# Three edits of one planning step in a fused attention and expert kernel: order of inverse roots, row copy and image differences on GpSimd, and a split wait on TensorE

## The chip, the cores and the metric

The kernel runs on one core of one Trainium2 chip. The metric is the device time of one launch in microseconds (us). Three runs of the kernel before gave 1237.05, 1237.48 and 1237.81 us; the median, 1237.48, is the time before. A smaller time is better.

## The reference

Sixteen images of 256 x 256 are turned into edge maps, 77 text rows are looked up in a table and set behind each, and the 333 x 256 sequence goes through windowed attention and a two-of-eight expert layer, each behind a layer norm and with a residual.

```python
def reference(x, x_txt, ...):
    h = _L0_tok_ref(x)          # clip(|x[i,j]-x[i+1,j+1]| + |x[i+1,j]-x[i,j+1]|, 0, 1)
    h = jnp.concatenate([h, _L0_txt_ref(L0_txt_weight, x_txt)], axis=1)
    h = h + _L0_attn_ref(_layernorm(h, axis=-1), Wq, bq, Wk, bk, Wv, bv, Wo, bo, pos_bias)
    h = h + _L0_ffn_ref(_layernorm(h, axis=-1), gate_w, w1, w2, w3)
    return h
# _layernorm: (x - mean) / sqrt(var + 1e-5)
# attention: 16 heads of 16; windows of 128 rows, every 64 rows, and one at the end; per window
#   softmax(q k^T / 4 + pos_bias) v, added up and divided by the number of windows over each row
# expert layer: softmax gate over 8 experts, the best two, silu(x w1) * (x w3) w2, weighted sum
```

## The kernel before

The program has two stages. The first, up to about 725 us, takes the images in a software pipeline; the second is a loop of expert tiles, which the change doesn't touch.

**Steps and slots.** Every engine runs the same outer loop over steps b = -3 to 17 and, in it, 20 slots k = 0 to 19 (5 windows x 4 groups of 4 heads). The order of the work is written out by hand: in slot k of step b an engine's code has the attention of image b and pieces of the images before and behind it. The flags say which pieces exist: `att` (image b is in attention), `tail` (image b-1 is being finished), `tail2` (image b-2 is sent to the expert slots), `proj` (image b+1 gets q, k and v), `inp` (image b+2 is normalised) and `pre` (image b+3 is made from pixels). So `pre` ends after step 12, `inp` after step 13 and `proj` after step 14. Engines meet only through semaphores; slots aren't barriers, and an engine that has nothing to wait for runs ahead.

**Attention in each slot.** TensorE computes the scores of group k (L1273), transposes the probabilities of group k-3 (L1284) and multiplies those of k-4 with the values (L1300). VectorE adds the bias and takes the maximum (L980), ScalarE takes the exponential (L741) and copies the transposed probabilities out of PSUM (L734); for one group in four VectorE makes that copy (L989), in slots 18, 2, 6, 10 and 14. Once per window TensorE turns the raw output (L753 on ScalarE, then L1409), VectorE scales it (L1001, L1008), TensorE turns it back (L1259, in slot 18 behind the gate matmuls), ScalarE copies it (L760) and GpSimd adds it into ctxT (L581).

**What the change touches, in slots 12 to 19.**
- GpSimd (`pool`), slot 12: the two image differences diag and anti (L631, L633), which wait for the pixels. Slot 13: `inverse_roots` (L506 to L518), 14 small instructions of which each waits for the one before; they wait for the statistics of the finished image b-1 (`ln2_step`) and of the coming image b+2 (`ln1_step`). Slot 15: ctxT (L581). Slot 16: the copy of the rows (L654), which waits for `rows0_ready`. Slot 18: h_res (L667), which waits for the normalised image b+2 (`xn_ready`), then the sum of the absolute differences (L672, waits for `conv_step`) and the clipped image (L677).
- VectorE (`dve`), slot 12: statistics of image b-1 (L810, L813). Slot 13: the absolute values of diag and anti (L1114). Slot 14: two of three value banks (`add_v`, L968). Slot 15: the rows of image b-1 (L818, three instructions, wait for `rstd_ready`). Slot 16: the third value bank (L968), then xn of image b+2 (L818, three). Slot 17: L980 and the scaling into ctx_q. Slot 18: L980 and the copy L989.
- TensorE (`pe`), slot 17: the transposes of the rows (L1390), six into the two halves of m_bank, behind one wait for the rows and one for all three values of image b+1, since these are read from m_bank. Slot 18: the gate matmuls (L1397), which wait for ScalarE's copy of these transposes (L728). Slot 0: the transposes of xn (L1329).
- SyncE loads the pixels of the next image when `diffs_ready` has counted the two differences.

## Time and profile before

| | |
|---|---|
| median of 3 runs | 1237.48 us |
| the profiled execution | 1235.95 us |
| its span, first to last instruction | 1233.8 us |
| TensorE busy (matmul) | 1146.1 us, 93% |
| VectorE busy | 837.9 us, 68% |
| ScalarE busy | 707.0 us, 57% |
| GpSimd busy | 595.6 us, 48% |
| one batch, L1409 to L1409, batches 2 to 12 | 40.9 us |

The profile is of one execution. Busy times are of instructions, without the waits; an engine's idle time is put down to what it waited for last. In the timelines below a line is one or several instructions of the same kind in a row: start, duration, engine, line of the code, what is written and read, how many, and in brackets the idle time before it and who ended it. GpSimd is called POOL, VectorE DVE, TensorE PE and ScalarE ACT. A batch is named by its step b.

### The profile page before, as it was taken

How to read it: one execution, taken by the hardware profiler on the slowest of the kernel's cores; microseconds unless marked ns; L12 is line 12 of the kernel's file. 1: busy time of each engine (PE TensorE's matmuls, PEld its weight loads, DVE VectorE, ACT ScalarE, POOL GpSimd, SP SyncE). 2: the span in 40 equal slices, each digit the busy share in tenths (PEclk: the TensorE clock that was granted, in tenths of full speed). 3: DMA queues.
4: the chain of work that ended last, by engine and by line, in shares of the span. 5: the costliest groups of instructions: out<-in, count | busy, mean ns of one | idle time of the engine just before them, and what ended most of it. 6: DMA issues, size and time to landing. Idle time of an engine off the chain costs nothing.

```text
span 1233.8 us, 34479 instructions
## 1 busy us (share of the span) xinstructions
PE 1146.1 (93%) x10510; PEld 944.6 (77%) x10511; DVE 837.9 (68%) x4279; ACT 707.0 (57%) x1979; POOL 595.6 (48%) x751
## 2 busy tenths in 40 slices
PE   2499999999999999999998798999999999999995
PEld 1366766676667667666766698999999999999995
DVE  3488899899989899989888774444444444444442
ACT  1399999999999999999999721111111111111110
POOL 7655656765676567656653362223232332323232
PEclk9799999999999999999999998999999999999998
DMA  4654446554554355434535332232333323233332
GB/s 134 180 162 122 139 136 188 142 147 131 153 144 114 96 151 147 111 99 129 148 99 173 112 101 45 47 47 47 48 47 50 47 47 47 47 47 49 49 47 30
DMA packets 98394, 123.31 MB, mean 100 GB/s; under 512 B 15544, under 2 KB 87416, under 8 KB 95192
## 3 DMA queue, kind: packets, MB, share of 16 engines
q1 hardware_dynamic: 75880, 89.96, 26.7%
q0 software_dynamic: 18576, 24.47, 12.0%
q10 hardware_dynamic: 3808, 7.34, 1.9%
q8 instruction: 59, 0.97, 0.3%
q14 instruction: 71, 0.58, 0.2%
HBM read 69.35 MB, written 46.07 MB: 94 GB/s over the span
## 4 chain that ended last, share of the span: by engine, by line
PE 70%; DVE 7%; ACT 7%; POOL 7%; issue 4%; SPq 2%; DMA 1%; ACTq 0%; POOLq 0%; DVEq 0%
PE t_bank L1197 13%; PE s_bank L1197 13%; PE o_bank L1212 13%; PE m_bank L1245 7%; PE t_bank L1284 6%; PE o_bank L1300 5%; ACT probs L741 4%; PE s_bank L1273 4%; DVE probs L980 3%; PE m_bank L1239 3%; PE m_bank L1397 2%; PE m_bank L1186 2%; PE o_bank L1259 1%; PE o_bank L1409 1%; ACT probsT L734 1%
## 5 line engine op out<-in xcount | busy, mean ns | idle before, releaser
L741 ACT ACTIVATE probs<-probs,neg_max 128x128 f32<-128x128 f32 x1280 | 402.4, 398 | 2.1 <-DVE neg_max L980 2.1
L980 DVE CUSTOM_DVE_ANT_0 probs<-s_bank,nbias 128x128 f32<-128x128 f32 x1280 | 293.4, 284 | 56.6 <-PE s_bank L1273 51.2
L699 ACT ACTIVATE v_all<-s_bank 128x512 f32<-128x512 f32 x91 | 54.4, 598 | 284.5 <-PE s_bank L1197 284.4
L1284 PE MATMUL t_bank<-ident,probs 128*128 128x128 f32 x1280 | 194.1, 274 | 0.2 <-ACT probs L741 0.2
L1212 PE MATMUL o_bank<-stacks,v_all 128*128 x728 | 172.7, 381 | 0.6 <-issue 0.5
L537 POOL DMA_INDIRECT out_dram<-wq_sb,nbias x46 | 75.0, 1629 | 176.5 <-DVE wq_sb L924 159.4
L734 ACT ACTIVATE probsT<-t_bank 128x512 f32<-128x512 f32 x240 | 142.0, 592 | 31.1 <-PE t_bank L1284 28.7
L537 POOL DMA_INDIRECT out_dram<-wk_sb,nbias x45 | 74.9, 1663 | 170.8 <-DVE wk_sb L924 161.9
L1212 PEld LDWEIGHTS o_bank<-stacks,v_all 128*128 128x128 f32 x728 | 131.6, 191 | 15.8 <-issue 1.7
L930 DVE TENSOR_TENSOR v_all<-v_all,t_bank 128x512 f32<-128x512 f32 x91 | 62.5, 687 | 119.0 <-PE t_bank L1197 119.0
L1300 PE MATMUL o_bank<-probsT,v_all 128*32 128x128 f32 x2560 | 136.3, 285 | 7.1 <-ACT probsT L734 4.0
L1273 PE MATMUL s_bank<-stacks 96*128 96x128 bf16 x1280 | 126.2, 221 | 16.7 <-DMA stacks<-qk_parts 16.7
L1273 PEld LDWEIGHTS s_bank<-stacks 96*128 96x128 bf16 x1280 | 93.6, 98 | 59.9 <-issue 24.8
L1284 PEld LDWEIGHTS t_bank<-ident,probs 128*128 128x128 f32 x1280 | 134.4, 141 | 0.8 <-ACT probs L741 0.5
L551 POOL DMA_INDIRECT expert_slots<-rows,slot_i x96 | 96.4, 1004 | 39.6 <-issue 39.6
L693 ACT ACTIVATE v_all<-m_bank 128x256 f32<-128x256 f32 x91 | 34.5, 383 | 131.5 <-PE m_bank L1186 131.5
L980 DVE DVE_READ_ACCUMULATOR2_ANT neg_max<- 128x1 f32 x1280 | 103.9, 81 | 0.0
L1300 PEld LDWEIGHTS o_bank<-probsT,v_all 128*32 128x32 f32 x2560 | 50.5, 108 | 62.3 <-issue 47.9
L1197 PEld LDWEIGHTS s_bank<-v_all,parts_flat 128*128 128x128 f32 x736 | 90.8, 195 | 4.0 <-ACT v_all L693 1.9
L1197 PE MATMUL s_bank<-v_all,parts_flat 128*128 128x128 f32 x736 | 91.7, 279 | 1.0 <-ACT v_all L693 1.0
L1197 PE MATMUL t_bank<-v_all,parts_flat 128*128 128x128 f32 x736 | 90.6, 277 | 0.0
L1197 PEld LDWEIGHTS s_bank<-v_all,probs 128*128 128x128 f32 x720 | 87.4, 192 | 2.3
(169 smaller groups left out, 1988.2 us busy)
## 6 DMA issues: line engine op xcount, KB each, us to landing
stacks<-qk_parts SPq DMA_DIRECT2D x192, 166.5 KB
qk_parts<-parts_flat SPq DMA_DIRECT2D x192, 83.2 KB
nbias<-expert_slots SPq DMA_DIRECT2D x91, 129.0 KB, 2.1
w_sb<-in_L_ffn_w_dram ACTq DMA_DIRECT2D x14, 512.0 KB, 3.8
v_all<-v_all SPq DMA_DIRECT2D x64, 96.0 KB
x_here<-in_x_dram SPq DMA_DIRECT2D x16, 256.0 KB
out_dram<-h_res SPq DMA_DIRECT2D x16, 256.0 KB
stacks<-in_L_ffn_w_dram SPq DMA_DIRECT2D x8, 512.0 KB, 6.0
```

What stands on the lines that cost most here:

```text
L537: pool.indirect_dma_start(out[:, :], bass.IndirectOffsetOnAxis(g_rows[r][:, D + 1:D + 2].bitcast(I32), 0), y_sb[r], None, compute_op=ALU.a ...
L551: pool.indirect_dma_start(slots_dram[:, :], bass.IndirectOffsetOnAxis(slot_i[0:n, kk, j:j + 1], 0), rows[0:n, kk, j, :], None).then_inc(sc ...
L734: act.activation(probsT[:, r, :], t_bank[:, r, :], ACT.Copy).then_inc(pT_by_act, 1)
L741: ins = act.activation(seg, seg, ACT.Exp, bias=neg_max[:, r, i:i + 1], scale=-1.0)
L930: dve.tensor_tensor(hidT[r % 2], hidT[r % 2], t_bank[:, r % 2, :], ALU.mult).then_inc(hid_ready, 1)
L980: ins = dve.tensor_tensor_reduce(probs[:, r, i * WIN:(i + 1) * WIN], s_bank[:, k % 2, i * WIN:(i + 1) * WIN], nbias[:, h, :], 1.0, BIG, AL ...
L1197: mm = pe.matmul(bank[:, par, n * P:(n + 1) * P], up_w[par][:, m, a, n * P:(n + 1) * P], gxT[par][:, a * P:(a + 1) * P], start=(a == 0), s ...
L1212: mm = pe.matmul(o_bank[:, r % 2, 0:D], hidT[r % 2][:, a * P:(a + 1) * P], w2_sb[:, bass.ds(e, 1), a, :].rearrange("p o n -> p (o n)"), st ...
L1245: mm = pe.matmul(m_bank[:, c, 0:S], (wq_sb if n == 0 else wk_sb)[:, a, c * P:(c + 1) * P], xT[:, a, :], start=(a == 0), stop=(a == C - 1))
L1273: mm = pe.matmul(s_bank[:, k % 2, i * WIN:(i + 1) * WIN], q_stack[par][0:KROWS, h, lo:lo + WIN], k_stack[par][0:KROWS, h, lo:lo + WIN], st ...
L1284: mm = pe.transpose(t_bank[:, (k - 3) % 2, i * WIN:(i + 1) * WIN], probs[:, r, i * WIN:(i + 1) * WIN], ident[:, :])
L1300: mm = pe.matmul(o_bank[32 * i:32 * i + 32, vp, g * WIN:(g + 1) * WIN], v_win[bp][:, w, c0:c0 + 2 * HD], probsT[:, (k - 4) % 2, i * WIN:(i ...
```

## The change

On GpSimd the inverse roots move from slot 13 to slot 12 (in steps from 0 on; before that they stay in 13), the row copy of slot 16 keeps its slot, and the image differences move from slot 12 to slot 16, behind the row copy (steps -3 and -1 keep slot 12, step -2 keeps 17). On VectorE the absolute values of the differences move from slot 13 to slot 17 in steps from 0 on. On TensorE the row transposes into the first half of m_bank wait for two of the three values and those into the second half for the third.

```diff
@@ gpsimd, step @@
-                    if pre and k == (17 if b == -2 else 12):
-                        pool.wait_ge(x_in, b3 * 64 + 64)
-                        ...
-                        pool.tensor_tensor(diag[:, :, :], x_here[:, :, 0:IMG], x_below[:, :, 1:IMG + 1],
-                                           ALU.subtract).then_inc(diffs_ready, 1)
-                        pool.tensor_tensor(anti[:, :, :], x_below[:, :, 0:IMG], x_here[:, :, 1:IMG + 1],
-                                           ALU.subtract).then_inc(diffs_ready, 1)
-                    if (tail or inp) and k == 13:
+                    if (tail or inp) and k == (13 if b < 0 else 12):
                         ...
                         inverse_roots(0 if inp else NT, 2 * NT if tail else NT, b + 2)
-                    if b == B and k == 14:
-                        pool.wait_ge(h2_stored, 32 * (B - 1))
-                        add_tile(0, 0)
                     if tail and k == 16:
                         pool.wait_ge(rows0_ready, b0 * 3 + 3)
                         if b0 >= 1:
                             pool.wait_ge(scattered, b0 * 96)
                         pool.tensor_copy(rows[:, 1, :, 0:D], rows[:, 0, :, 0:D]).then_inc(rows1_ready, 1)
+                    if pre and k == (17 if b == -2 else 12 if b < 0 else 16):
+                        pool.wait_ge(x_in, b3 * 64 + 64)
+                        ...
+                        pool.tensor_tensor(diag[:, :, :], x_here[:, :, 0:IMG], x_below[:, :, 1:IMG + 1],
+                                           ALU.subtract).then_inc(diffs_ready, 1)
+                        pool.tensor_tensor(anti[:, :, :], x_below[:, :, 0:IMG], x_here[:, :, 1:IMG + 1],
+                                           ALU.subtract).then_inc(diffs_ready, 1)
+                    if b == B and k == 14:
+                        pool.wait_ge(h2_stored, 32 * (B - 1))
+                        add_tile(0, 0)
@@ vector, step @@
-                    if pre and k == (17 if b == -2 else 13):
+                    if pre and k == (13 if b in (-3, -1) else 17):
                         for i, side in enumerate((diag, anti)):
@@ tensor, step @@
                     if tail and k == 17:
                         pe.wait_ge(rows0_ready, b0 * 3 + 3)
                         if b == B:
                             pe.wait_ge(gxT_ready, 4)
-                        if proj:
-                            pe.wait_ge(v_ready, b1 * 3 + 3)
                         for c in range(C):
+                            if proj:
+                                pe.wait_ge(v_ready, b1 * 3 + 2 + c)
                             for j, (t0, n) in enumerate(TILES):
```

The `add_tile(0, 0)` of step 16 keeps its slot 14; it only stands elsewhere in the text.

## Rows read from the trace of the kernel before

**Rows 1.** The page, part 1: busy time, share, instructions.
```profile
PE 1146.1 (93%) x10510; PEld 944.6 (77%) x10511; DVE 837.9 (68%) x4279; ACT 707.0 (57%) x1979; POOL 595.6 (48%) x751
```

**Rows 2.** The waits: engine, line, awaited; us in total, times, longest.
```profile
DVE rows L818 <- POOL rstd L518: 8.6, 11, 0.8
...
PE m_bank L1390 <- DVE v_all L968: 7.7, 11, 0.7
```

**Rows 3.** Timeline of TensorE, batch 8, slots 16 to 18.
```profile
446.60 0.66 PE L1409 MATMUL o_bank<-ident,raw 128*128 128x128 f32 x4 [0.32 <-ACT raw L753]
...
448.99 0.77 PE L1390 MATMUL m_bank<-ident,rows 128*128 128x128 f32 x6 [0.70 <-DVE v_all L968]
...
450.71 1.34 PE L1397 MATMUL m_bank<-gate_sb,rest 128*128 128x8 f32 x12
```

**Rows 4.** Timeline of TensorE, batch 13, slots 16 to 2.
```profile
610.26 0.66 PE L1409 MATMUL o_bank<-ident,raw 128*128 128x128 f32 x4 [0.32 <-ACT raw L753]
...
611.87 0.80 PE L1390 MATMUL m_bank<-ident,rows 128*128 128x128 f32 x6
...
614.17 1.33 PE L1397 MATMUL m_bank<-gate_sb,rest 128*128 128x8 f32 x12 [0.47 <-ACT rest L728]
...
616.37 0.43 PE L1300 MATMUL o_bank<-probsT,v_all 128*32 128x128 f32 x8
...
621.52 0.43 PE L1300 MATMUL o_bank<-probsT,v_all 128*32 128x128 f32 x8 [0.29 <-ACT probsT L734]
```

**Rows 5.** Timeline of ScalarE, batch 13, slots 18 and 19.
```profile
613.40 0.72 ACT L728 ACTIVATE rest<-m_bank 128x666 f32<-128x666 f32 x1
...
616.97 1.27 ACT L741 ACTIVATE probs<-probs,neg_max 128x128 f32<-128x128 f32 x4
```

**Rows 6.** Timeline of GpSimd, batch 8, slots 12 to 18.
```profile
439.73 1.10 POOL L631 TENSOR_TENSOR diag<-x_here,x_below 128x512 f32<-128x512 f32 x1
440.78 1.09 POOL L633 TENSOR_TENSOR anti<-x_below,x_here 128x512 f32<-128x512 f32 x1
441.96 0.58 POOL L506 TENSOR_SCALAR var_eps<-moments 128x6 f32<-128x6 f32 x1
...
446.14 0.72 POOL L581 TENSOR_TENSOR ctxT<-ctxT,head_out 128x256 f32<-128x256 f32 x1
...
449.89 1.81 POOL L667 TENSOR_TENSOR h_res<-h_in,bo_row 128x768 f32<-128x768 f32 x1 [1.34 <-DVE xn L818]
```

**Rows 7.** Timeline of GpSimd, batch 13, slots 13 to 16.
```profile
603.95 0.24 POOL L506 TENSOR_SCALAR var_eps<-moments 128x6 f32<-128x6 f32 x1 [0.58 <-issue]
...
609.77 0.82 POOL L654 COPY rows<-rows 128x768 f32<-128x768 f32 x1 [1.25 <-DVE rows L818]
```

**Rows 8.** Timeline of VectorE, batch 13, slots 16 to 19.
```profile
610.80 1.04 DVE L818 TENSOR_SCALAR xn<-w_sb,moments,rstd 128x256 f32<-128x256 f32 x3
...
613.32 0.28 DVE L980 CUSTOM_DVE_ANT_0 probs<-s_bank,nbias 128x128 f32<-128x128 f32 x1
...
614.15 0.69 DVE L989 COPY probsT<-t_bank 128x512 f32<-128x512 f32 x1
616.04 0.29 DVE L980 CUSTOM_DVE_ANT_0 probs<-s_bank,nbias 128x128 f32<-128x128 f32 x1 [1.20 <-PE s_bank L1273]
```

**Rows 9.** Timelines of VectorE and GpSimd, steps 8 and -2: instructions side by side.
```profile
446.22 0.80 DVE L818 TENSOR_SCALAR rows<-h_res,moments,rstd 128x256 f32<-128x256 f32 x1 [0.78 <-POOL rstd L518]
...
442.08 0.41 DVE L1114 TENSOR_SCALAR anti<-anti 128x512 int32<-128x512 int32 x1
...
20.94 1.29 DVE L1114 TENSOR_SCALAR diag<-diag 128x512 int32<-128x512 int32 x1 [1.25 <-POOL diag L631]
...
20.86 1.08 POOL L633 TENSOR_TENSOR anti<-x_below,x_here 128x512 f32<-128x512 f32 x1
```

**Rows 10.** Timelines of TensorE and GpSimd, batch 0, slots 18 and 19.
```profile
84.68 0.42 PE L1300 MATMUL o_bank<-probsT,v_all 128*32 128x128 f32 x8 [0.25 <-DVE probsT L989]
...
81.71 1.85 POOL L667 TENSOR_TENSOR h_res<-w_sb,bo_row 128x768 f32<-128x768 f32 x1 [3.16 <-DVE xn L818]
```

More of the change, by code:

```diff
@@ L624, in step @@
                         scatter(1, 2)
-                    if pre and k == (17 if b == -2 else 12):
-                        pool.wait_ge(x_in, b3 * 64 + 64)
-                        if b == -2:
-                            pool.wait_ge(xn_ready, 3)
-                        if b3 >= 1:
-                            pool.wait_ge(image_ready, b3)
-                        pool.tensor_tensor(diag[:, :, :], x_here[:, :, 0:IMG], x_below[:, :, 1:IMG + 1],
-                                           ALU.subtract).then_inc(diffs_ready, 1)
-                        pool.tensor_tensor(anti[:, :, :], x_below[:, :, 0:IMG], x_here[:, :, 1:IMG + 1],
-                                           ALU.subtract).then_inc(diffs_ready, 1)
-                    if (tail or inp) and k == 13:
+                    if (tail or inp) and k == (13 if b < 0 else 12):
                         if tail:
@@ L654, in step @@
                         pool.tensor_copy(rows[:, 1, :, 0:D], rows[:, 0, :, 0:D]).then_inc(rows1_ready, 1)
+                    if pre and k == (17 if b == -2 else 12 if b < 0 else 16):
+                        pool.wait_ge(x_in, b3 * 64 + 64)
+                        if b == -2:
+                            pool.wait_ge(xn_ready, 3)
+                        if b3 >= 1:
+                            pool.wait_ge(image_ready, b3)
+                        pool.tensor_tensor(diag[:, :, :], x_here[:, :, 0:IMG], x_below[:, :, 1:IMG + 1],
[5 more added lines that the diff above has]
+                        add_tile(0, 0)
                     if b == B and k == 17:
```

## The prediction

> **What bounds the kernel now.** I read the page first: TensorE is busy for 1146.1 us, 93% of the span, no other engine for more than 838 [rows 1]. A change that only moves work on VectorE and GpSimd can therefore win no more than TensorE's own idle time, and it can lose wherever it makes TensorE wait. The view of the waits says how much of that idle time is of the kind aimed at: the transposes of the rows (L1390) wait for the value bank (L968) in 11 batches, 7.7 us in all, and VectorE's normalisation (L818) waits for the inverse roots (L518) in 11, 8.6 us [rows 2]. The timeline of batch 8 shows one such place: 0.70 us of idle before L1390, and none before the gate matmuls L1397 that follow [rows 3].
>
> The best evidence is in the trace itself. Batches 13 and 14 have no image to prepare, so POOL issues no differences and VectorE no absolute values there; in batch 13 the roots already stand directly behind their statistics. There L1390 starts without idle time. But 0.47 us of idle appears before L1397 [rows 4], because ScalarE can copy the transposed rows (L728) only at 613.40, behind its exponentials [rows 5]. From the transposes of the raw heads (L1409) to L1397 it is 450.71 - 446.60 = 4.11 us in batch 8 and 614.17 - 610.26 = 3.91 us in batch 13 [rows 3, 4]. So a removed stall of 0.70 us is worth 0.20 us a batch: ScalarE is next. I use batch 13 as the model of a changed batch and give its times as they stand in the trace.
>
> **The change part by part.**
>
> *Roots earlier.* Steps b = 0 to 12 have both differences and roots in slot 12/13 (16 images, three of them prepared before step 0). Taking the two differences, 2.1 us from 439.73 to the end of the second at 441.87 [rows 6], from in front of the 14 root instructions makes the roots end some 2.2 us sooner. VectorE's wait for them (8.6 / 11 = 0.78 us [rows 2]) goes, the rows are written sooner, and the value bank with them. In the model the roots start at 603.95, against a start at 441.96 in batch 8 [rows 6, 7]: counted from L1409 that is 6.31 us ahead of it instead of 4.64, and without the stretched first instruction. The rows are there for POOL's row copy at 609.77 [rows 7]. Worth 11 x 0.20 = 2.2 us, batches 2 to 12; batch 1 has no stall at L1390 today, as the 11 of the waits say [rows 2]. That is also all that can be had there: the time behind it is ScalarE's.
>
> *Bank by bank.* The first half of the transposes needs v_ready to have counted two instead of three. In the model even the third value is early enough: no idle time before L1390 at 611.87 [rows 4]. Splitting the wait is worth 0; its bounds are 0 and what the model's third value could be late by, at most today's 0.70 us. The added wait stands on TensorE's queue in front of three transposes and all that follows; it is met by then, so 0; the most I would grant it is the 0.05 us that I estimate for a semaphore step from VectorE to TensorE. The row copy keeps its place behind the rows, so the scatters of the next step find it ready. In steps -3 to -1 the code leaves the order as it is. The image load of SyncE waits for the differences, some 0.7 us later than now at most; the data is needed a whole batch later, in slot 16, so it costs 0.
>
> *The differences at their new place.* This is where I expect the price. They follow the row copy, so in the model they run from 609.77 + 0.82 = 610.59 to about 612.7 (two at the pitch 440.78 - 439.73 = 1.05 us) [rows 6, 7]. In the middle of this VectorE starts the three normalisations of xn, at 610.80 [rows 8]. Do VectorE and POOL disturb each other? Three rows say so. The first normalisation at 446.22 takes 0.80 us, while three that nothing holds take 1.04 together; POOL's addition into ctxT runs beside it from 446.14 to 446.86 [rows 6, 8, 9]. The absolute value at 20.94 takes 1.29 us instead of 0.41, while POOL's anti difference runs from 20.86 to 21.94 [rows 9]. In the other direction POOL's var_eps takes 0.58 us under the two absolute values, against 0.24 in batch 13 [rows 6, 7]. So such instructions exclude one another for the length of an instruction. The two differences and the three normalisations (1.04 us together) then need 2.1 + 1.0 = 3.1 us one after the other, in whichever order: both are done at about 613.7 instead of xn at 611.8.
>
> The Trainium skill (SBUF — State Buffer, Who interferes with whom) says that an instruction in a two-port mode, or a GpSimd one, takes the shared port pair "for the whole instruction"; the trace agrees, with 0.80 us for one held normalisation against 1.04 for three free ones. The same page says that a VectorE instruction with one input outside these modes does not contend. The normalisation takes about 0.35 us for 256 elements, the absolute value 0.41 as a whole for 512 [rows 8, 9], so one could take the former for an instruction at single rate that POOL leaves alone: that is the first rival below. The held row of 0.80 us speaks against it.
>
> *The addition behind them.* POOL's h_res (L667, 1.81 us [rows 6]) waits for all of xn and follows at once: 613.7 to 615.5.
>
> *The absolute values in slot 17.* They leave slot 13, where VectorE had them between two softmax steps and TensorE had no idle time to lose, so nothing is won there. They now stand between the ctx_q scaling and the softmax step of slot 18, which begins at 613.32 in the model [rows 8]. VectorE has room behind it: 1.20 us of idle before 616.04 [rows 8], and the pair costs 0.7 to 0.8 (twice 0.41, overlapping by some 0.07 [rows 9]). With nothing held the pair would be free. But VectorE arrives late from the held xn, between 614.2 (it gets the port right after the first difference) and 615.2 (POOL first), and then meets h_res. In every order it waits until 615.5. From batch 8: POOL's anti ends at 441.87, the second of the held absolute values starts at 442.08 and takes 0.41 [rows 6, 9], and the next instruction starts some 0.07 before it ends, at 442.42: 0.55 us behind POOL. So slot 18's softmax begins at 616.05 and its copy of the probabilities (L989) 0.83 later (614.15 - 613.32), at 616.9; it takes 0.69, and TensorE's L1300 starts a semaphore step behind it, at 617.65. In the model L1300 starts at 616.37 [rows 4]. The stall is 1.28 us. Of this 0.29 is given back at 621.52, where TensorE waits for ScalarE anyway [rows 4]: 1.0 us a batch. ScalarE's next input from VectorE, the maxima of slot 18, is ready at 616.9, just when ScalarE begins on them at 616.97 [rows 5]. VectorE is 1.5 us late there, but each thing that TensorE takes from it in the next slots comes over 1 us ahead of need, by the distances in the timelines. Bounds of this term: 0 (if the 1.20 us swallow it) and 2 us (if the lateness adds up with a second wait).
>
> *Batch 0* has no rows, and its differences are over before xn. But h_res runs from 81.71 for about 1.8 us, and the absolute values come inside it; TensorE waits for L989 there already, 0.25 us [rows 10], so up to 1.0 us of lateness reaches it. Between 0 and 1.0 I take 0.6.
>
> **The sum.** -11 x 0.20 + 12 x 1.0 (batches 1 to 12) + 0.6 = +10.4 us. Against the profiled execution's own 1235.95 us (a span of 1233.8 and 2.15 us around it) that is 1246.4; the median of the runs is 1.5 us above the profiled one, so 1247.9 us.
>
> **Rivals.**
> *Nothing is held (0.20).* The normalisations of xn run beside the differences, or the port changes hands so quickly that little is lost. Then h_res runs from 612.7 to 614.5, the absolute values that come at 613.32 are through at 615.1, the copy of the probabilities ends at 616.6, and TensorE's 0.29 us swallow the rest. The price of the differences is gone, and the 2.2 us are won: 1235.3 us. For it: the 1.20 us of VectorE's idle. Against it: the 0.80 and 1.29 us rows. It decides as soon as slot 18's softmax begins before 614.8 in the model, from where L1300 is on time.
> *The full stall comes back (0.03).* ScalarE's place before L1397 does not bind, for instance because its exponentials start earlier: 11 x 0.70 = 7.7 us, 1229.8 us. Batches 13 and 14, with their 0.47 us, say no.
> *Half of it (0.12).* xn is held, but the absolute values are not held by h_res, or come before it: slot 18 begins between 614.9 and 615.9, the stall is 0.1 to 1.1 us, in the middle 0.3 us net a batch: 1237.5 - 2.2 + 4 = about 1239 to 1245, say 1241.
> *The lateness piles up (0.07).* The maxima of slot 17 come to ScalarE after 614.0, and VectorE's 1.5 us reach TensorE in slots 0 to 2 as well: 2 us a batch, 1237.5 - 2.2 + 24 = 1259 us.
>
> **How the numbers follow.** The forecast has 0.58. Its own range is a third of a microsecond a batch either way, 1244 to 1252. The 80% range must reach down to the first rival, so 1234.6 to 1252; left out are the piled-up case, the full stall and the edges. A measurement of this kernel can tell about 0.2%, 2.5 us, from no change, so the first rival, -2.2 us, lies mostly within it. Faster: 0.03 and a part of 0.08 of the first rival, 0.11. Same: the rest of it and the edge of the half case, 0.16. Slower: 0.73.
>
> **What would show each step.** In the changed kernel's timeline of a batch from 2 to 12: no idle before L1390, 0.4 to 0.5 us before L1397 <- ACT rest (roots, right). The first or second xn normalisation at 0.7 us or more (the hold, right; all three in 1.04: first rival). The first absolute value at over 0.8 us with its end behind h_res's. An idle time of 1.0 to 1.4 us before slot 19's L1300 <- DVE probsT. The distance from one batch's L1409 <- ACT raw to the next at 41.7 us (40.91 now, 40.71 behind batch 13). The prediction is wrong if the distance is below 41.2, and wrong in its mechanism if it is above with the 1.29 us kind of row missing.

## The result, and the profile after

The change makes the kernel slower by 0.31%: 1240.21 us (median of 10 runs, 1238.96 to 1241.73) against 1236.24 us (10 runs of before on the same chip), ratio 1.0031, 95% interval 1.0023 to 1.0040, which is +3.97 us. The forecast had the sign, but it asked for +10.4 us. Executions that took about twice as long or more (2419.76 us once for before on the chip of e1 to e4, 2852.62 and 4908.41 us in e9) are left out of every median here. The profiled execution took 1241.54 us with a span of 1239.4, 5.6 us above the span before; it lies 1.3 us above the median of its own kernel, so the traces show a little more than the medians do.

The page of the kernel after, part 1, answers [rows 1]:

```profile
PE 1148.3 (93%) x10510; PEld 946.8 (76%) x10511; DVE 847.9 (68%) x4279; ACT 708.5 (57%) x1979; POOL 591.4 (48%) x751
```

VectorE is busy 10.0 us longer with the same 4279 instructions: it does no more work, but some instructions take longer. The view of the waits of the kernel after (us in total, times, longest), against [rows 2]:

```profile
PE o_bank L1300 <- DVE probsT L989: 13.5, 17, 1.5
...
PE m_bank L1397 <- ACT rest L728: 7.4, 15, 0.7
```

and the same two rows of the kernel before:

```profile
PE o_bank L1300 <- DVE probsT L989: 2.9, 5, 1.5
...
PE m_bank L1397 <- ACT rest L728: 2.1, 4, 0.7
```

Both waits of [rows 2] are gone. In their place stand a wait of L1397 for ScalarE (+5.3 us in 11 more places) and one of L1300 for VectorE (+10.6 us in 12 more places). TensorE's timeline of batch 12 shows them. (By the count of steps the batch of before that starts at 446.60 us and is called batch 8 in the rows is batch 9: batch 13 starts at 610.26, four times 40.91 us behind it. Nothing hangs on the name, since L1397 stands 4.10 to 4.14 us behind L1409 in each batch from 2 to 12.) The timeline begins at L1409, as [rows 4] does, so 35.14 us are to be added to a time for the frame of the model batch 13 (610.26 - 575.12):

```profile
575.12 0.66 PE L1409 MATMUL o_bank<-ident,raw 128*128 128x128 f32 x4 [0.32 <-ACT raw L753]
...
576.74 0.80 PE L1390 MATMUL m_bank<-ident,rows 128*128 128x128 f32 x6
...
579.03 1.33 PE L1397 MATMUL m_bank<-gate_sb,rest 128*128 128x8 f32 x12 [0.47 <-ACT rest L728]
...
582.12 0.43 PE L1300 MATMUL o_bank<-probsT,v_all 128*32 128x128 f32 x8 [0.81 <-DVE probsT L989]
```

No idle time before L1390; 0.47 us before L1397, and L1397 is 3.91 us behind L1409: the model batch to the hundredth. Then 0.81 us before slot 19's L1300. VectorE and GpSimd in the same batch:

```profile
575.66 2.42 DVE L818 TENSOR_SCALAR xn<-h_in,moments,rstd 128x256 f32<-128x256 f32 x3
...
579.55 0.73 DVE L1114 TENSOR_SCALAR diag<-diag 128x512 int32<-128x512 int32 x1
580.21 0.41 DVE L1114 TENSOR_SCALAR anti<-anti 128x512 int32<-128x512 int32 x1
...
581.38 0.68 DVE L989 COPY probsT<-t_bank 128x512 f32<-128x512 f32 x1
```

```profile
575.43 1.08 POOL L648 TENSOR_TENSOR diag<-x_here,x_below 128x512 f32<-128x512 f32 x1
576.47 1.13 POOL L650 TENSOR_TENSOR anti<-x_below,x_here 128x512 f32<-128x512 f32 x1
578.16 1.84 POOL L667 TENSOR_TENSOR h_res<-w_sb,bo_row 128x768 f32<-128x768 f32 x1 [0.55 <-DVE xn L818]
```

The three normalisations of xn take 2.42 us beside the differences, against 1.04 [rows 8], and it is 2.42 or 2.43 us in every batch from 1 to 12. The first absolute value takes 0.73 us beside h_res, against 0.41 unheld [rows 9], and ends 0.28 us behind it (580.28 against 580.00). The copy of slot 18's probabilities, and with it L1300, is late. From one L1409 to the next (the period) it is 41.03 to 41.07 us in batches 3 to 12 (one of 41.39), against 40.91 before.

Where did the 5.6 us of the spans come from? Over batches 0 to 13 the starts of L1409 give it piece by piece. From batch 3 to the end of batch 12: 410.89 us against 409.19, +1.70. Batch 0: 39.02 against 38.97, +0.05. Batch 2: 42.40 against 40.91, +1.49, and batch 1: 43.75 against 40.72, +3.03. The last two don't fit the others, and they are more than half of it. In the view of stretches (us, busy time of each engine, PEclk, DMA share, GB/s) the kernel after has

```profile
125.00:130.00 5.00, 4.21 (x35) 2.87 (x33) 4.41 (x39) 4.09 (x12) 3.35 (x4) 0.57 0.39 123
130.00:135.00 5.00, 5.00 (x46) 3.63 (x45) 3.47 (x24) 3.50 (x10) 0.00 (x0) 0.74 0.58 169
...
170.00:175.00 5.00, 5.00 (x50) 3.70 (x50) 3.81 (x37) 4.04 (x12) 2.24 (x3) 0.66 0.35 121
```

where the kernel before has

```profile
125.00:130.00 5.00, 4.89 (x64) 3.59 (x62) 4.55 (x42) 4.71 (x13) 1.80 (x3) 1.00 0.67 220
```

TensorE's granted clock falls to half, 1.2 GHz in place of 2.4, for 6.8 us from 125.7 and for 3.4 us from 170.1; the text calls this half clock. The timeline shows it on one operation, four transposes into t_bank that take 0.60 us, then 1.06:

```profile
124.73 0.60 PE L1284 MATMUL t_bank<-ident,probs 128*128 128x128 f32 x4
126.13 0.65 PE L1300 MATMUL o_bank<-probsT,v_all 128*32 128x128 f32 x8 [0.79 <-DVE probsT L989]
...
127.11 1.06 PE L1284 MATMUL t_bank<-ident,probs 128*128 128x128 f32 x4
```

In both batches TensorE has two idle times beside the 0.32 us before L1409: 0.47 to 0.48 us before L1397 and 0.79 to 0.82 before L1300. The first fall lies within the second of them (125.34 to 126.13), the other 0.2 us behind it. An undisturbed batch, one without half clock, of this kernel takes 41.06 us, so the stretches cost 43.75 - 41.06 = 2.69 and 42.40 - 41.06 = 1.34 us. What is left of the 6.27 us over batches 0 to 13, 2.24, are the stalls.

### The profile page after: what moved, and what is told of

Read it like the earlier page. It is cut to its first block, busy times and chain, and to the rows that moved or that the text cites. A ratio compares the mean times of both kernels' runs of the same rounds, so it can differ in the third digit from the quotient of the medians.

```text
span 1239.4 us, 34479 instructions
## 1 busy us (share of the span) xinstructions
PE 1148.3 (93%) x10510; PEld 946.8 (76%) x10511; DVE 847.9 (68%) x4279; ACT 708.5 (57%) x1979; POOL 591.4 (48%) x751
## 4 chain that ended last, share of the span: by engine, by line
PE 77%; DVE 13%; issue 3%; ACT 3%; SPq 2%; DMA 2%; POOL 1%; DVEq 0%; POOLq 0%; ACTq 0%
PE t_bank L1197 13%; PE s_bank L1197 13%; PE o_bank L1212 13%; PE t_bank L1284 7%; PE m_bank L1245 7%; PE o_bank L1300 6%; PE s_bank L1273 5%; DVE probs L980 4%; PE m_bank L1239 4%; PE m_bank L1251 3%; PE o_bank L1409 2%; DVE xn L818 2%; PE m_bank L1186 2%; ACT probs L741 2%; PE o_bank L1259 1%
## 5 line engine op out<-in xcount | busy, mean ns | idle before, releaser
L1300 PE MATMUL o_bank<-probsT,v_all 128*32 128x128 f32 x2560 | 137.2, 287 | 14.0 <-DVE probsT L989 13.5
L980 DVE DVE_READ_ACCUMULATOR2_ANT neg_max<- 128x1 f32 x1280 | 107.5, 86 | 0.0
L1300 PEld LDWEIGHTS o_bank<-probsT,v_all 128*32 128x32 f32 x2560 | 50.5, 108 | 69.6 <-issue 49.2
```

Source lines behind the costliest of these rows:

```text
L980: ins = dve.tensor_tensor_reduce(probs[:, r, i * WIN:(i + 1) * WIN], s_bank[:, k % 2, i * WIN:(i + 1) * WIN], nbias[:, h, :], 1.0, BIG, AL ...
L1300: mm = pe.matmul(o_bank[32 * i:32 * i + 32, vp, g * WIN:(g + 1) * WIN], v_win[bp][:, w, c0:c0 + 2 * HD], probsT[:, (k - 4) % 2, i * WIN:(i ...
```

## The experiments

They ran on three chips: e1 to e4 on one where the kernel before takes 1236.10 us (28 runs), e5 to e8 on a second (1242.57 us, 15 runs), e9 to e11 on a third (1243.34 us, 29 runs). Ratios are always to before on the same chip, with a 95% interval in brackets. Line numbers are those of each kernel; beside an edit they shift by the lines it adds.

**e1_after_again: the kernel after, unaltered.** No edit.

> The changed kernel unaltered, as the measure for the three others on this chip. Theory: VectorE comes 0.8 us late to the copy of slot 19's matmuls (L1300 <- DVE probsT 0.8 us in batches 1 to 12), of which TensorE gives back some 0.57 us at two places where it waited for ScalarE before; 0.34 us a batch remain against the unstalled pace of 40.71 us, so 41.05 us from L1409 to L1409. That makes 12 x 0.34 - 11 x 0.20 = 1.9 us over the kernel before; the rest of the measured 4 us is TensorE's clock, which was granted at half for 6.8 us behind batch 1 and 3.4 us behind batch 2 in the profile of the changed kernel and not in that of the one before. Expected: 3 to 5 us over before, 41.05 us again in the profile, and half-clock stretches again in the early batches. Rival (the half-clock stretches were an accident of one execution): the profile shows 41.05 us but no such stretch, and the median is still 4 us over before.

1240.68 us, ratio 1.0035 [1.0022, 1.0048]. Half clock comes again in batches 1 and 2, now 3.4 us from 127.9 and 6.8 us from 168.9; undisturbed batches take 41.03 to 41.08 us (one 41.39 again), with 0.78 to 0.83 us before L1300. The second fall comes ahead of that batch's idle time before L1300, behind 0.60 us of idle before L1259. So the early stretches are no accident of one execution. They are not in every execution to the same extent either: the mean granted clock over the span is 0.983 in both profiled executions of this kernel, but 0.986 in nine of the ten executions of the result and in one of the five here.

**e2_split_only: the kernel before with the split wait, nothing moved.**

```diff
-                        if proj:
-                            pe.wait_ge(v_ready, b1 * 3 + 3)
                         for c in range(C):
+                            if proj:
+                                pe.wait_ge(v_ready, b1 * 3 + 2 + c)
```

> The kernel before with the split wait alone. The prediction priced the split at 0 since in the whole change the third value is early. Alone it has something to hide: the rows are ready at 447.66 and TensorE is free at 448.29 in batch 8, so the first three transposes need not wait, and only the second three wait until 448.99. L1390 then ends 0.38 us sooner and the gate matmuls are limited by ScalarE's copy, which can start at 449.74: L1397 at about 450.55 instead of 450.71. Expected 0.15 us a batch in 11 batches, 1.7 us under before. Rival (a wait between two matmul groups costs what it saves): 0, within 0.5 us of before.

1233.88 us, ratio 0.9985 [0.9977, 0.9994]: faster than before and after. TensorE in batch 9, against [rows 3]:

```profile
447.97 0.51 PE L1390 MATMUL m_bank<-ident,rows 128*128 128x128 f32 x3
448.67 0.51 PE L1390 MATMUL m_bank<-ident,rows 128*128 128x128 f32 x3 [0.19 <-DVE v_all L968]
...
450.27 1.33 PE L1397 MATMUL m_bank<-gate_sb,rest 128*128 128x8 f32 x12
```

The roots still come late (the rows' normalisations wait 0.79 us for them), but only the second half of the transposes waits, 0.19 us, and L1397 starts 3.91 us behind L1409, ScalarE's time. The period is 40.71 to 40.73 us in every batch from 1 to 13. The edit that the prediction put at nothing wins alone all that the prediction expected of the roots in front, and the two don't add up: with the split alone L1397 stands at 3.91 us behind L1409, and with both edits, in the kernel after, at 3.91 again, where ScalarE's copy sets it. The roots moved without the split were not run.

**e9_split_again: the same kernel on the third chip, more runs.**

> The kernel before with the split wait alone, once more and with more rounds. If it is worth what the first look said, and what the moved roots are worth at best (11 batches by 0.70 us before L1390 less the 0.47 us at L1397 that ScalarE sets): -11 x 0.20 = -2.2 us, between -1.4 and -2.6, ratio 0.998 to 0.999. Period from L1409 to L1409 40.72 us, no stretch of half clock between batch 0 and batch 14. Rival (the first look was luck of the chip): ratio 0.9995 to 1.0005.

1241.16 us (ten runs), ratio 0.9981 [0.9972, 0.9990]. The gain holds: 2.2 us by the medians on either chip. On this chip the period is less even, 40.71 to 41.08 us, with 0.32 to 0.57 us of idle before L1390 left in 3 batches.

**e3_abs_behind_copy: the kernel after, absolute values behind slot 18's copy of the probabilities.**

```diff
-                    if pre and k == (13 if b in (-3, -1) else 17):
+                    if pre and k == (13 if b in (-3, -1) else 17 if b < 0 else 18):
                         for i, side in enumerate((diag, anti)):
```

> The changed kernel with the absolute values behind slot 18's copy of the probabilities instead of ahead of slot 18's softmax; nothing else moves. Theory (the price is what stands ahead of that copy: the hold of the absolute values by h_res and their own 0.8 us): the normalisations of xn stay held (2.4 us for the three), but the copy ends about 1.0 us sooner, L1300 waits 0.1 us or less, 40.72 us a batch from 1 to 12; 2 us under before and some 6 us under the changed kernel, with no half-clock stretch in the early batches. Rival (the held normalisations alone are the price): L1300 still waits 0.4 us or more and the time stays at or over before.

1236.85 us, ratio 1.0004 [0.9995, 1.0013]. The stall before slot 19's L1300 is gone, and so is the early half clock. VectorE in batch 12: xn still held, the absolute values free behind the copy.

```profile
571.29 2.42 DVE L818 TENSOR_SCALAR xn<-h_in,moments,rstd 128x256 f32<-128x256 f32 x3
...
576.03 0.69 DVE L989 COPY probsT<-t_bank 128x512 f32<-128x512 f32 x1
576.63 0.42 DVE L1114 TENSOR_SCALAR diag<-diag 128x512 int32<-128x512 int32 x1
```

The time is that of before, where 2 us less were expected, and the period is 40.92 to 41.00 us (one of 41.29), not the 40.72 expected. TensorE runs with the model up to slot 2's L1300, 11.26 us behind L1409 in both. Then the transposes of ctx_q in slot 2 start 11.92 us behind L1409, against 11.73 in batch 13 of before, and the batch stays 0.2 us late:

```profile
582.68 0.44 PE L1259 MATMUL o_bank<-ident,ctx_q 128*128 128x128 f32 x2
```

ctx_q (L1008) is ready at 582.13 + 0.49. So VectorE's lateness does reach TensorE a second time, three slots on. The prediction said that it wouldn't.

**e4_diffs_behind_hres: differences behind h_res in slot 18, absolute values behind slot 18's copy.**

```diff
-                    if pre and k == (17 if b == -2 else 12 if b < 0 else 16):
+                    if pre and k == (17 if b == -2 else 12) and b < 0:
...
+                    if pre and k == 18 and b >= 0:
+                        ...
```

> Roots in slot 12 and split wait as in the change, differences behind h_res in slot 18, absolute values behind slot 18's copy. Theory: nothing of VectorE's is held in slot 16 (three normalisations in 1.05 us), VectorE waits for the second difference until about 1 us after its copy, slot 19's softmax is 0.3 us late at most and that is hidden: 40.71 us a batch, 2 us under before, the same as with the absolute values behind the copy alone within 0.5 us. Rival (a later image delays the gather and the addition into ctxT that stand behind it on GpSimd, or VectorE's 0.3 us at slot 19 reach TensorE): above 40.8 us a batch, slower than with only the absolute values moved.

1236.24 us, ratio 0.9994 [0.9984, 1.0005]. xn takes 1.05 us again, and the period is 40.71 to 40.73 us in the undisturbed batches: the theory's part is right. Two batches take 41.8 and 42.2 us. GpSimd in the second of them, then VectorE, then TensorE:

```profile
451.75 1.81 POOL L667 TENSOR_TENSOR h_res<-h_in,bo_row 128x768 f32<-128x768 f32 x1 [2.72 <-DMA out_dram<-h_res]
...
454.65 1.30 DVE L1124 TENSOR_SCALAR diag<-diag 128x512 int32<-128x512 int32 x1 [1.36 <-POOL diag L676]
...
457.36 0.77 PE L1339 MATMUL m_bank<-ident,xn 128*128 128x128 f32 x6 [0.99 <-DVE logits L1151]
461.93 0.44 PE L1269 MATMUL o_bank<-ident,ctx_q 128*128 128x128 f32 x2 [1.01 <-DVE ctx_q L1018]
```

h_res waits for the store that still reads its buffer, and the differences behind it inherit the wait. A half clock of 3.4 us at 669.5, behind the batches, comes on top. The place is right in ten of the 12 batches, and a DMA that comes late in two takes the gain in this execution. It was the slowest of the twelve (1238.84 us; the fastest took 1231.72), so it doesn't say how often that happens. In the batch shown TensorE is idle for 0.47, 0.99 and 1.01 us, and the clock stays at 2.4 GHz.

**e5_tiny_abs: the kernel after, absolute values on 4 elements a partition.**

```diff
-                            bits = side[:, :, :].bitcast(I32)
+                            bits = (side[:, :, :] if b < 0 else side[:, :, 0:2]).bitcast(I32)
```

> The changed kernel with absolute values of 4 elements per partition instead of 512 in steps from 0 on; the rest of the image keeps its signs, so this part of the computation is left out. It keeps the wait for the port and takes the work of 0.66 us away. Theory (the hold by h_res is the larger part): the tiny absolute value comes at the same place, ctx_q's end, and still waits for h_res to end; slot 18's softmax starts some 0.5 us sooner than in the changed kernel, L1300 waits 0.2 to 0.4 us instead of 0.80, and since two of TensorE's waits for ScalarE give that back, 40.75 to 40.9 us from L1409 to L1409. Rival (the work is the price and the hold is not): the first absolute value takes under 0.2 us, L1300 does not wait.

This kernel leaves a part of the computation out. It ran once (1243.70 us), so there is no ratio. The stall before slot 19's L1300 is 0.40 to 0.43 us in eight batches and 0.26 to 0.29 in the other four, not 0.81. Even with nothing to do the first of the pair is held by h_res, which ends at 453.33:

```profile
451.52 1.81 POOL L667 TENSOR_TENSOR h_res<-h_in,bo_row 128x768 f32<-128x768 f32 x1 [0.55 <-DVE xn L818]
...
452.91 0.45 DVE L1114 TENSOR_SCALAR diag<-diag 128x4 int32<-128x4 int32 x1
453.27 0.16 DVE L1114 TENSOR_SCALAR anti<-anti 128x4 int32<-128x4 int32 x1
...
454.92 0.43 PE L1300 MATMUL o_bank<-probsT,v_all 128*32 128x128 f32 x8 [0.40 <-DVE probsT L989]
```

So about half of the stall is the pair's own work and half is lateness from the held xn and the wait for h_res. The period is 40.71 to 40.89 us in eight of the 12 batches, like that of the kernel without any stall (e7, below): a stall of 0.4 us costs almost nothing. Two are at 41.1 us, and two near 42 us have half clock (from 125.9 and 371.7, 3.4 us each); these two are the ones with the smallest stall, 0.26 us.

**e6_diffs_behind_roots: differences in slot 13, right behind the roots.**

```diff
+                    if pre and k == 13 and b >= 0:
+                        ...
-                    if pre and k == (17 if b == -2 else 12 if b < 0 else 16):
+                    if pre and k == (17 if b == -2 else 12) and b < 0:
```

> The changed kernel with the differences in slot 13, right behind the roots, so that they are over before the normalisations of xn; the absolute values stay in slot 17. Theory: the differences run from about 2.6 us to 0.5 us before L1409. They hold at least one normalisation of the rows (slot 15, 1.5 us before L1409), by up to 1 us, but the rows are due only at L1390; xn is not held (1.05 us for three), h_res runs from 2.7 to 4.5 us behind L1409 and holds the absolute values from 3.1 to 4.5: slot 18's softmax 0.6 us sooner than in the changed kernel, L1300's wait 0.2 us, below what is given back; but slot 2's L1259 may come 0.2 us late as it does with the absolute values behind the copy. 40.72 to 40.95 us a batch; the time between -0.2% and 0 of before. Rival (the rows, held, come late to L1390): idle time at L1390 of 0.3 us or more and 41 us a batch.

A clear miss: 1252.18 us, ratio 1.0076 [1.0062, 1.0090], the slowest of the places tried for the differences. GpSimd and VectorE in batch 9:

```profile
451.87 1.09 POOL L643 TENSOR_TENSOR diag<-x_here,x_below 128x512 f32<-128x512 f32 x1
452.92 1.14 POOL L645 TENSOR_TENSOR anti<-x_below,x_here 128x512 f32<-128x512 f32 x1
...
452.31 2.62 DVE L828 TENSOR_SCALAR rows<-h_res,moments,rstd 128x256 f32<-128x256 f32 x3
...
456.04 1.05 DVE L828 TENSOR_SCALAR xn<-w_sb,moments,rstd 128x256 f32<-128x256 f32 x3
457.17 1.81 POOL L677 TENSOR_TENSOR h_res<-h_in,bo_row 128x768 f32<-128x768 f32 x1 [1.34 <-DVE xn L828]
```

xn is free, 1.05 us. But the roots release three normalisations of the rows, of the same size, and the differences, right behind the roots, run just beside those: 2.62 us. Everything on VectorE behind them is late: the value bank (0.22 us before L1390), xn, and through xn h_res, which now ends at 458.98, 5.14 us behind L1409, against 4.88 in the kernel after (580.00 - 575.12). The absolute values meet it as in the kernel after, and the stall is 1.06 to 1.10 us in nine batches:

```profile
461.10 0.43 PE L1310 MATMUL o_bank<-probsT,v_all 128*32 128x128 f32 x8 [1.06 <-DVE probsT L999]
```

The period is mostly 41.3 to 41.5 us where the clock is full, and half clock comes three times in the batches, at 168.8, 336.1 and 503.3.

**e7_tiny_both and e10_tiny_both_again: differences and absolute values both on 4 elements a partition.** This kernel, called the tiny kernel below, leaves the image part of the computation out.

```diff
+                        w = IMG if b < 0 else 2
-                        pool.tensor_tensor(diag[:, :, :], x_here[:, :, 0:IMG], x_below[:, :, 1:IMG + 1],
+                        pool.tensor_tensor(diag[:, :, 0:w], x_here[:, :, 0:w], x_below[:, :, 1:w + 1],
```

(the same for anti and for the absolute values)

> The changed kernel with both the differences and the absolute values on 4 elements per partition in steps from 0 on; this leaves the image part of the computation out. Nothing is held and nothing late. Theory: every batch from 1 to 12 runs at the pace that batch 13 has in the kernel before, 40.72 us, no wait at L1300 in slot 19, no half-clock stretch in the early batches; 2.3 us under before, the bound on what earlier roots can give. Rival (the roots' new place costs something of its own): above 40.8 us.

1240.39 us, ratio 0.9984 [0.9974, 0.9993]. The repeat:

> The kernel after with differences and absolute values on 4 elements a partition in batches 0 to 12 (the rest is left out). The zero of the dose, on this chip: both theories expect a period of 40.7 to 40.9 us, no idle time at slot 19's L1300, 0.29 us <- ACT probsT in slot 2, no early half clock, ratio 0.9975 to 0.9995.

1242.27 us, ratio 0.9988 [0.9979, 0.9997]. In both profiles the whole price of the moved work is gone: slot 19's L1300 starts without idle time (one batch of e7 has 0.20 us), and no half clock comes between batches 0 and 13. What remains is 2.2 us by the medians in e7 and 1.1 in e10, no more than the split alone wins (2.2 us in e2 and e9); what the moved roots give alone can't be told from it. The period is 40.70 to 40.91 us, 40.85 or more in 16 of 24 batches, where 40.72 was expected; some 0.15 us appear ahead of one L1300 about 31 us behind L1409. The tiny work isn't the cause: batch 13, which no edit touches, takes 40.85 to 40.89 us in all of e5 to e11, e9 among them, and 40.71 to 40.73 in before, after and e1 to e4. It comes with the two later chips, and why is not explained.

**e8_tiny_late_4 and e11_tiny_late_3: the lateness without the hold.** The tiny kernel, with sums over 512 elements on VectorE in slot 17, four in e8 and three in e11; their results are not used.

```diff
+                    if pre and b >= 0 and k == 17:
+                        for i in range(4):
+                            dve.tensor_reduce(spare[:, i:i + 1], nbias_flat[:, 0:512], AX.X, ALU.add)
```

> The kernel with tiny differences and absolute values, and in slot 17, where the absolute values stand, four sums over 512 elements each of a constant tile on VectorE (about 2.4 us; their results are unused), in steps 0 to 12. It makes VectorE as late as it is in the changed kernel (2.36 us at slot 18's softmax by batch 12, against batch 13) without any use of the shared port. Theory (only the lateness counts): L1300 waits about 1.0 us for DVE probsT, and 41.1 to 41.3 us from L1409 to L1409; the same half-clock stretches in the early batches as in the changed kernel, since TensorE's idle places are the same. Rival (the port itself, or GpSimd's lateness, is what costs): the pace stays under 40.9 us. Rival for the clock (the half-clock stretches come with something else): no stretch in batches 1 to 3.

1257.41 us, ratio 1.0107 [1.0086, 1.0128]. The four sums take 2.46 us:

```profile
464.76 2.46 DVE L1114 TENSOR_REDUCE spare<-nbias 128x1 f32<-128x512 f32 x4
...
468.85 0.42 PE L1305 MATMUL o_bank<-probsT,v_all 128*32 128x128 f32 x8 [1.07 <-DVE probsT L991]
...
469.61 1.06 PE L1289 MATMUL t_bank<-ident,probs 128*128 128x128 f32 x4
```

The stall is 1.07 us, the period 41.5 us where the clock is full, above the 41.1 to 41.3 expected, and half clock comes near the stall in six batches. The sums are not held: four take 2.46 us, 0.62 each, and the three of e11 1.85 us, 0.62 each too, though h_res runs beside the first ones (464.51 to 466.32 here). So a VectorE that is late is enough for the stall and for half clock in the early batches; the hold matters in the kernel after in that it makes VectorE late.

> The same as the tiny kernel, with three sums of 512 elements on VectorE in slot 17 (about 1.85 us; four of them took 2.46 us and gave a stall of 1.07 us at slot 19's L1300): 0.61 us less lateness, so a stall of 0.45 to 0.5 us. What does TensorE give back of it? If 0.57 us (0.29 at slot 2's L1300 and 0.28 ahead of slot 0's L1409, behind ScalarE), the period is that of the tiny kernel within 0.05 us, and of 12 x 0.48 = 5.8 us of stall less than 1 us is left in the time. If only the 0.29 us of the prediction's sum, the period is 0.2 us longer and the time 2.3 us. Stretches of half clock: if they come from TensorE's idle time at slot 19 alone, few or none here (0.4 us was followed by two at most in another kernel, 1.07 by six); each counts 1.3 to 2.7 us beside.

1247.35 us, ratio 1.0038 [1.0024, 1.0051], +5.1 us over e10, more than expected. TensorE in batch 11:

```profile
537.80 0.43 PE L1305 MATMUL o_bank<-probsT,v_all 128*32 128x128 f32 x8 [0.50 <-DVE probsT L991]
...
539.29 0.80 PE L1334 MATMUL m_bank<-ident,xn 128*128 128x128 f32 x6
539.92 0.60 PE L1414 MATMUL o_bank<-ident,raw 128*128 128x128 f32 x4
...
542.37 0.43 PE L1305 MATMUL o_bank<-probsT,v_all 128*32 128x128 f32 x8
```

against a batch of e10:

```profile
535.25 0.80 PE L1330 MATMUL m_bank<-ident,xn 128*128 128x128 f32 x6
536.17 0.66 PE L1410 MATMUL o_bank<-ident,raw 128*128 128x128 f32 x4
...
538.91 0.43 PE L1301 MATMUL o_bank<-probsT,v_all 128*32 128x128 f32 x8 [0.28 <-ACT probsT L735]
```

A stall of 0.50 us is paid back by slot 2. From L1330 to L1410 it is 0.92 us in e10, and 0.63 between the same two in e11; and the 0.28 us before slot 2's L1301 is gone. Counted from its L1409, slot 2's L1300 stands at 11.26 to 11.27 us in both, and L1259 behind it only 0.03 us later in e11. Over the ten batches without half clock in them or just ahead the period is 40.89 us against 40.81 in e10: of 12 stalls of 0.5 us about 0.9 us is left in the time, as expected ("less than 1 us"), and not the 2.3 us more that 0.29 us of slack would give. The difference of 0.08 us is within the scatter of the periods on this chip; the positions in the batch are the firmer evidence. The rest of the 5.1 us is batch 0 (2.16 us before L1300 in place of 0.72; the batch takes 39.96 us, not 38.96) and half clock: once in the batches, 3.4 us at 372.4, and behind them once more than in e10 (669.3) and for 10.2 us in place of 6.8 near 750.

## Why the prediction was right or wrong

The chain of causes was forecast as it came: xn held, h_res late, the absolute values held, L1300 late. The step that failed is the size of its price, the term of 1.0 us a batch (1.28 us of stall less 0.29 given back): it measured 0.34 us a batch against the unstalled pace. L1300 was late by 0.89 us, not 1.28, and 0.70 us came back by slot 2, not 0.29; 0.14 us came on top at ctx_q. Half clock, which the prediction didn't have, added to the time.

**Roots earlier: right.** No idle time before L1390, 0.47 or 0.48 us before L1397 in batches 1 to 13, 3.91 us from L1409 to L1397. e7 and e10 leave 2.2 and 1.1 us when the price is taken away, against the 2.2 forecast. But these kernels have the split wait too, and the split alone gives as much.

**Bank by bank: worth 0 only beside the moved roots.** That is how the prediction priced it. Its bound ("at most today's 0.70 us") had the answer of e2 in it, but the question was not asked the other way round: alone it makes the kernel 2.2 us faster on both chips (0.9985 and 0.9981), and then the moved roots are the edit that adds nothing.

**The hold of xn: right, its length too long.** The three normalisations took 2.42 us, against 1.04 in [rows 8]. The prediction took 3.1 us for differences and normalisations together (2.1 + 1.0). From the start of the first difference to the end of the last normalisation they took 578.08 - 575.43 = 2.65. The single normalisations start at 575.66, 576.58 and 577.68 and show 1.00, 1.18 and 0.40 us: the first comes through between the two differences, the second behind both, and anti grew by only 0.04 us (1.13 against 1.09 in [rows 6]). The first normalisation cost GpSimd almost nothing, so adding the busy times counted 0.45 us that isn't there. The Trainium skill (SBUF — State Buffer, Who interferes with whom) says that whoever issues first has the shared pair for the whole instruction; the row of xn bears out the waiting, but the 0.04 us of anti are far less than the 0.35 us that a normalisation takes, so in the other direction no hold of a whole instruction shows.

**h_res and the absolute values: right, 0.4 us sooner.** h_res ended at 580.00, which is 615.14 in the model's frame, not 615.5. The held absolute value, the second of 0.41 us and the softmax behind them came as the prediction had them. Slot 18's copy of the probabilities began at 616.52, not 616.9, and L1300 at 7.00 us behind L1409 (617.26), not at 617.65: late by 0.89, with 0.81 us of idle before it, not 1.28.

**What is given back: the term that was sized worst.** The prediction let TensorE make up 0.29 us. These are the starts counted from L1409 (model batch 13 of before, then batch 12 of after): slot 19's L1300 6.11 and 7.00, late by 0.89; slot 0's L1409 8.51 and 9.12, late by 0.61; slot 2's L1300 11.26 and 11.45, late by 0.19. So 0.70 us comes back, 0.28 of it ahead of slot 0's L1409 and 0.42 from there to slot 2's L1300, where the prediction had 0.29. The slack ahead of L1409 stands in no row of TensorE's matmuls. It shows only in the row of the weight loads, here of the kernel before in batch 9:

```profile
454.40 0.60 PEld L1329 LDWEIGHTS m_bank<-ident,xn 128*128 128x128 f32 x6 [0.20 <-issue]
455.31 0.42 PEld L1409 LDWEIGHTS o_bank<-ident,raw 128*128 128x128 f32 x4 [0.31 <-ACT raw L753]
```

and after, in batch 12, the wait is gone:

```profile
583.60 0.60 PEld L1329 LDWEIGHTS m_bank<-ident,xn 128*128 128x128 f32 x6 [0.20 <-issue]
584.17 0.43 PEld L1409 LDWEIGHTS o_bank<-ident,raw 128*128 128x128 f32 x4
```

e11 is the test of it: a stall of 0.50 us, made without any hold, is gone at slot 2's L1300.

**"Each thing that TensorE takes from it in the next slots comes over 1 us ahead": wrong.** ctx_q of slot 2 does not. L1259 starts 12.06 us behind L1409 in the kernel after against 11.73 in the model, so the 0.19 us of lateness grow to 0.33. e3 shows it alone: no stall at L1300, and still 0.2 us a batch at L1259. This step erred the other way and hid a part of the first two errors. The distances that the prediction read were those of a VectorE that is on time; behind 1.4 us of hold and the moved pair it runs without a pause to slot 2.

**Batch 0: sized too high.** The idle time before L1300 grew from 0.25 to 1.25 us, as the prediction's upper end had it, but the batch takes only 0.05 us more, not 0.6: the next two waits that TensorE had there in the kernel before, slot 0's L1409 <- ACT raw (0.38 us) and slot 2's L1300 <- ACT probsT (0.28), are gone. The delay is 0.99 us at L1300 (5.20 against 4.21 behind L1409), 0.45 at slot 0's L1409 and 0.05 at slot 2's L1300.

**The sum again.** 12 x 0.34 (41.05 - 40.71) - 11 x 0.20 + 0.05 = +1.9 us by the rounded terms, +2.24 by the starts themselves. Forecast by the same count: 12 x 1.0 - 2.2 + 0.6 = 10.4. By its numbers the case is the prediction's third rival, "half of it": slot 18's softmax began at 615.68 in the model's frame, inside its 614.9 to 615.9, at 0.3 us net a batch, and its 1241 us is near the 1240.21 measured. That nearness is luck: the absolute values were held by h_res, which that rival denies; its sum as written, 1237.5 - 2.2 + 4, is 1239.3 and not 1241; and the measured time has half clock in it, which no rival has. The forecast put 0.58 on the other case because it added up the instructions of the two engines as if none could slip in between others, and counted the slack from the matmuls' idle times alone.

**Half clock: missing from the prediction.** It is 4.0 of the 6.3 us in the profiled execution, which had more of it than most. Its mean granted clock is 0.983, against 0.986 in the nine other executions of the kernel after and 0.987 in the profiled one of before. Its 10.2 us at half clock take 0.004 off the mean, a single stretch of 3.4 us would take 0.0014, so the others have room for about one. The medians agree: +3.97 us less 2.24 of stalls leaves some 1.7 us, an estimate, where one stretch cost 1.34.

In the profiles the kernels with 0.8 us and more before L1300 (after, e1, e6, e8) all have such stretches between batches 0 and 13; before, e2, e3, e4, e7, e9 and e10, without that stall, have none there. e5 and e11, with stalls of 0.3 to 0.5 us, have two and one. That is a tendency and no rule. The kernel before is idle for 0.70 us before L1390 in 11 batches, and e4 for 1.0 us twice in one, and their clock stays up there. After has half clock in batches 1 and 2 in both profiled executions and then ten stalls of the same length without it. The executions without a trace blur it further: four of the twelve of e2 have a mean clock of 0.984 (its profiled one 0.987) and take 2.4 us longer than the other eight by the medians, and five of the ten of e10 have 0.981 or 0.982 (profiled 0.986), though these kernels have no such stall. Where their stretches lie is not known. What decides whether and in which batch half clock comes stays open.

## What to carry to other kernels

Ask of each part of a change what it is worth alone and what it is worth behind the others: here one small edit, the split wait, had all the gain that the runs show, the moved roots added none to it, and the moved differences brought the cost. Before a stall is booked, look for what comes after it: waits of the matmuls, waits of the weight loads (they show on a row of their own), and the next value taken from the engine that is late. Work on GpSimd that reads and writes large tiles has to be placed against every large VectorE instruction nearby, not only the one it was moved away from (e6).

## What the runs showed of the hardware

- Between two GpSimd subtractions issued back to back (1.08 and 1.13 us, against 1.10 and 1.09 unheld) one normalisation of 128 x 256 on VectorE slips in: 1.00, 1.18 and 0.40 us for the three, and 0.04 us for GpSimd.
- A VectorE instruction on 4 elements a partition is held by h_res on GpSimd as one on 512 is: 0.45 us in e5 against 0.16 for the next, ending with h_res (453.36 against 453.33).
- VectorE's sums of 128 x 512 are not held by h_res: 0.62 us each in e8 and e11, beside it or behind it.
- TensorE's granted clock fell from 2.4 to 1.2 GHz, for 3.4 or 6.8 us at a time, behind idle times as short as 0.48 and 0.79 us (after) or 0.47 and 0.26 us (e5) within one batch, though in after the engine was 96% busy in the 20 us before (19.20 of 20.00 us from 105 to 125). In after they cost 1.34 and 2.69 us, more than the 0.34 us a batch that the stall itself cost. Idle times of 0.99 and 1.01 us in one batch of e4 were followed by none.
- A chip can matter more than the change: the kernel before took 1236.1 us on one and 1242.6 and 1243.3 us on two others.
